# A graph network's attention loop: transposes and a small product moved to the end of a step, a row normalisation moved one step on

## The reference, cut to what matters

```python
    os1 = ssp(os1)                          # layer 3, scalar part; ssp(x) = softplus(x) - log 2
    os2 = os1 @ w_f2o2_s / math.sqrt(B)     # "the scalars' second product", B = 128
    ...                                     # x3 = layernorm(x2 + layer 3)
    q, k, v = jnp.split(x @ W, [Fqk, 2 * Fqk], axis=-1)      # layer 4, x is x3, H = 8 heads
    aw = jnp.einsum('ehf,ehf->eh', q[src] * scaling, k[dest])
    m = jax.ops.segment_max(aw, src, num_segments=n)
    e = jnp.exp(aw - m[src])
    denom = jax.ops.segment_sum(e, src, num_segments=n)
    out = jax.ops.segment_sum((e / denom[src])[:, :, None] * v[dest], src, num_segments=n)
x = _layernorm(x + out)
```

## Time and profile before

| | us |
|---|---|
| median of 3 runs | 2155.89 |
| lowest, highest | 2150.03, 2163.36 |
| the profiled execution's own time | 2165.3 |
| its span, first to last instruction | 2163.5 |
| PE busy | 1853.0 (86%) |
| DVE busy | 1442.2 (67%) |
| ACT busy | 1157.3 (53%) |

### The profile page before, as it was taken

How to read it: one execution, slowest core, us unless ns; L and a number is a source line. 1 busy time by engine, 2 the same in 40 slices (tenths; PEclk the granted TensorE clock), 3 DMA queues, 4 the chain that set the end, 5 groups by cost and what they waited for, 6 DMA issues and landing times. The chain is left out here.

```text
span 2163.5 us, 24571 instructions
## 1 busy us (share of the span) xinstructions
PE 1853.0 (86%) x5525; PEld 953.6 (44%) x5525; DVE 1442.2 (67%) x2642; ACT 1157.3 (53%) x2376; POOL 916.6 (42%) x1049
## 2 busy tenths in 40 slices
PE   5999999599999999999999995952881878888885
PEld 2444444244444444444444443521781444444442
DVE  5365555077777777777777774327985687788774
ACT  1344434255555555555555552224884888778772
POOL 2212102156666666666666663444553222232214
PEclk9999999799999999999999998975555887787777
DMA  7752102534444444444444445554556877777743
GB/s 251 246 206 67 25 10 31 141 133 171 171 164 164 158 164 171 171 167 161 167 156 171 171 147 199 98 93 156 113 111 189 244 223 222 223 221 215 225 133 119
DMA packets 165550, 344.68 MB, mean 159 GB/s; under 512 B 30146, under 2 KB 30627, under 8 KB 164966
## 3 DMA queue, kind: packets, MB, share of 16 engines
q1 hardware_dynamic: 130710, 247.28, 32.6%
q0 software_dynamic: 31424, 92.08, 19.0%
q10 hardware_dynamic: 3344, 4.51, 0.7%
HBM read 171.91 MB, written 153.71 MB: 151 GB/s over the span
## 5 line engine op out<-in xcount | busy, mean ns | idle before, releaser
L687 PE MATMUL d_p_h<-w3a,d_xT 128*128 128x512 f32 x632 | 286.4, 596 | 23.1 <-DMA d_xT<-in_xT 23.1
L687 PE MATMUL d_p_o<-d_w,d_uT 128*128 128x512 f32 x632 | 284.5, 593 | 3.0 <-ACT d_uT L762 3.0
L687 PE MATMUL d_p_p<-d_wr,d_x1T 128*128 128x512 f32 x632 | 285.1, 594 | 0.0
L562 POOL TENSOR_SCALAR d_small<-d_mv 128x1 f32<-128x1 f32 x158 | 78.0, 494 | 297.5 <-DVE d_mv L813 149.5
L851 DVE TENSOR_TENSOR d_zz<-d_yg,d_xbeta 128x512 f32<-128x512 f32 x79 | 136.9, 1733 | 96.2 <-POOL d_yg L902 96.2
L687 PEld LDWEIGHTS d_p_h<-w3a,d_xT 128*128 128x128 f32 x632 | 120.9, 192 | 176.0 <-issue 176.0
L687 PEld LDWEIGHTS d_p_o<-d_w,d_uT 128*128 128x128 f32 x632 | 119.8, 190 | 153.8 <-issue 149.2
L755 ACT ACTIVATE d_yn<-d_y,d_small 128x512 f32<-128x512 f32 x79 | 64.3, 814 | 228.4 <-POOL d_small L567 228.4
L1739 PE MATMUL f_p_qv<-filters,same_dst 128*128 128x512 f32 x160 | 126.4, 962 | 66.8 <-ACT same_dst L1819 66.8
L687 PEld LDWEIGHTS d_p_p<-d_wr,d_x1T 128*128 128x128 f32 x632 | 114.5, 191 | 114.4 <-issue 114.4
L783 ACT ACTIVATE d_x<-d_zz,d_small 128x512 f32<-128x512 f32 x79 | 64.2, 813 | 176.6 <-POOL d_small L567 176.6
(11 more groups left out here) (285 smaller groups left out, 4110.3 us busy)
## 6 DMA issues: line engine op xcount, KB each, us to landing
sum_counted<-m_tile_sum SPq DMA_DIRECT2D x10, 2112.0 KB, 7.8
state<-d_empty SPq DMA_DIRECT2D x80, 264.0 KB, 2.4
update<-d_empty SPq DMA_DIRECT2D x80, 256.0 KB, 2.3
pair_x<-x SPq DMA_DIRECT2D x40, 512.0 KB, 4.2
out_rows<-pair_rows SPq DMA_DIRECT2D x40, 512.0 KB, 3.7
d_xT<-in_xT SPq DMA_DIRECT2D x79, 256.0 KB, 2.7
d_z<-sum_counted SPq DMA_DIRECT2D x79, 256.0 KB, 2.8
d_x<-in_x SPq DMA_DIRECT2D x79, 256.0 KB, 3.1
```

The source lines that it names most:

```text
L562: nc.gpsimd.tensor_scalar(tmp, var, factor, add, ALU.mult, ALU.add).then_inc(done, 1)
L687: last = nc.tensor.matmul(out[:, :], lhsT[:, c, :], w[:, c, :], start=(c == 0), stop=(c == KB - 1))
```

## The change

On PE, the softplus transpose and the second product are now those of tile `a` (in the step in which its softplus is made), and the x3 transposes are those of tile `b` (in the step in which the rows are normalised). All of them stand after the keys and ahead of the tile sums. On ACT, their copies stand after `x3_rows(b)`, ahead of the step's last `tile_normalise`. `source_rows` runs for tile `e - 1`, one step later than before, and stands right after `state_factors(e)`. No instruction is added or removed; DVE, POOL and SP keep their lists.

```diff
@@ tensor
-                b, c, d = step - 1, step - 2, step - 3
-                if 0 <= c < T:
-                    turn_x3(c, 0)
-                    turn_x3(c, 1)
-                if 0 <= b < T:
-                    turn_ssp(b)
+                a, b, c, d = step, step - 1, step - 2, step - 3
                 if 0 <= c < T:
...
                     queries(c)
                 if 0 <= d < T:
                     turn_scores(d)
-                if 0 <= b < T:
-                    second(b)
-                if 0 <= d < T:
                     spread_scores(d)
                     values(d)
                 if 0 <= c < T:
                     keys(c)
+
+                if a < T:
+                    turn_ssp(a)
+                if 0 <= b < T:
+                    turn_x3(b, 0)
+                    turn_x3(b, 1)
+                if a < T:
+                    second(a)
                 if 0 <= d < T:
                     tile_sums(d)
@@ scalar
                 if 0 <= d < T:
                     away_from(d)
-                if 0 <= c < T:
-                    x3_turned_out(c, 0)
-                    x3_turned_out(c, 1)
                 if 0 <= e < T:
                     state_factors(e)
-                if 0 <= b < T:
-                    ssp_turned_out(b)
+                if 0 <= e - 1 < T:
+                    source_rows(e - 1)
...
                 if 0 <= d < T:
                     scores_out(d)
-                if 0 <= b < T:
-                    second_product_out(b)
...
                     x3_rows(b)
-                if 0 <= e < T:
-                    source_rows(e)
+                if a < T:
+                    ssp_turned_out(a)
+                if 0 <= b < T:
+                    x3_turned_out(b, 0)
+                    x3_turned_out(b, 1)
+                if a < T:
+                    second_product_out(a)
                 for u in range(unit + early + between, unit + TILES[step]):
                     tile_normalise(nc, k, act, u)
```

## The result

| | before | changed |
|---|---|---|
| median, us | 2156.65 (4 runs, 2150.03 to 2163.36) | 2223.61 (4 runs, 2223.36 to 2226.96) |
| ratio of the times | | 1.0314, 95% interval 1.028 to 1.0348 |
| profiled execution, us | 2165.3 | 2223.53 |
| span, us | 2163.5 | 2221.8 |

The kernel became slower, by the mechanism that was forecast and by more than was forecast: 2206 was predicted, with a range up to 2220, and 2223.61 came.

A forecast was written before the change was run, and what follows sets the result against it. Bound: PE's wait for ACT's x3 copies, behind DVE's attended row, in a 23.87 us step. +48 over 16 steps, +4 and -2 at the ends make +50: 2215 on the profiled execution, 2206 us on the median's footing; range 2174 to 2220.

The forecast's parts named there:

- The bound before, and the wait that goes: PE at the queries: 3.7 us of idleness and 6.7 of queries leave the critical chain, if nothing else were late.
- ACT's factors are late next: ACT at the factors: waits 1.6 us a step for DVE's f_fall, which ends 9.64 us after the weighing.
- Queued behind the factors: ACT from factors to score copy: 7.44 us, so the spread starts no sooner than 17.1 after the weighing.
- The clock behind it: PE after a 7.5 us gap: spread 3.5 and values 6.1 at low clock, period 26.9, +48 over 16 steps.
- The ends: Outside the sixteen steps: +4 us for the step ahead of them, -2 at the other end.
- The sum and its footing: Whole kernel: +48 + 4 - 2 = +50; 2215 us on the profiled 2165.3, 2206 on the median of 2155.89.
- The range: Whole time: 2174 to 2220 us; values between 5.19 and 6.56 and a spread between 3.0 and 4.0 give 2183 to 2222.
- A: Rival, PE's clock stays up in the loop: period 22.8 us, a gain of 17, time 2137; chance 0.06.
- B: Rival, the removed wait is paid out as factors are ready when ACT comes: step 20.5 us, time 2102; chance 0.07.
- C: Rival, only the values on PE are slow, not the spread, or values rise soonest: period 24.5 us, time 2168; chance 0.09.

The follow-up runs named there:

- Experiment 1: Changed kernel with one swap on ACT: source rows of the step before stand ahead of the factors instead of behind them; 2191.93 us, ratio 1.0145 to the kernel before.
- experiment 2: Changed kernel with source rows put back to tile e, right behind the x3 rows, moved transposes kept; 2192.95 us, ratio 1.014 to the kernel before.
- experiment 6: Kernel before with only the source rows one step later, behind the factors; transposes and second product not moved; 2217.73 us, ratio 1.0253.
- experiment 3: Changed kernel plus 14 unread products of 256 columns on PE between score transpose and spread; 2184.85 us, ratio 1.0106 to the kernel before.
- experiment 7: Changed kernel plus 17 unread products on PE in the gap ahead of the spread; 2172.76 us, ratio 1.0049 to the kernel before.
- experiment 8: Changed kernel with ACT reordered: query and score copies right behind the factors, then source rows and two plain tiles, two tiles at the end; 2149.35 us, ratio 0.9941.
- experiment 9: The new ACT order of experiment 8 with the plain tiles half a step sooner; 2121.66 us, ratio 0.981 to the kernel before.

## Why the prediction was right or wrong, point by point

- **The bound before, and the wait that goes.** Right: PE's wait at the queries went, and the queries run at full clock, from 5.66 to 9.26 us after the weighing (5.7 to 9.2 forecast).
- **ACT's factors are late next.** Right: 1.57 us a step, 1.6 forecast. Experiment 1 removed the wait by order alone and moved the spread by the source rows' 1.6.
- **Queued behind the factors.** Right: the spread comes 17.04 after the weighing (17.1), in experiments 1, 2 and 6 at 15.45, 15.62 and 17.30 (15.4, 15.6, 17.3).
- **The clock behind it.** The mechanism is right (experiments 3 and 7). Two terms of the sum were low: the spread took 3.71, not 3.5, and the values 6.36, not 6.1. That makes a period of 27.31 instead of 26.9, and over the 16 steps +55.1 (2156.77 - 1719.76 = 437.0 against 381.9) where the sum had +48. The slow spread lies between its bounds of 2.0 and 4.0; it was scaled from a spread of which only the last 0.71 us ran slowly. The estimate of 3.8 worked out from the ratio of 1.91 for 128 columns (the Trainium skill, "TensorE: Matmul & The Clock Gate", section "Back-to-back issue gap") was nearer: 3.71 / 1.98 is 1.87.
- **The ends.** This step failed most for its size: +2 was forecast, +9.2 came. *Start:* +4 was forecast. From the first logarithms (1654.73 before, 1648.72 after) to the first of the 17 spreads it took 64.1 before and 71.0 after: +6.9. The step that was priced came near, 24.26 instead of 19.77, +4.5. The other 2.4 lie ahead of its spread (44.4 and 46.8 us from the logarithms) and were not in the sum. There ACT now stands at the end of a step waiting for PE's slow transposes and second product, where plain tiles lay between before. In the first step of the changed kernel:

```profile
1651.59 0.38 ACT L1836 ACTIVATE f_sspT<-f_p_O 128x256 f32<-128x256 f32 x1 [1.56 <-PE f_p_O L1723]
1653.29 0.39 ACT L1842 ACTIVATE f_y<-f_p_R 128x256 f32<-128x256 f32 x1 [1.31 <-PE f_p_R L1733]
```

  The first of these waits is in the kernel before too, also 1.56; the second is new, and so are three short ones in each of the next two steps, 0.75 a step. Two waits of the kernel before, 0.35 and 0.66, are gone. That is 1.8 more of waiting, and one copy more stands ahead of the first spread.

  *End:* -2 was forecast, +2.3 came (62.7 us from the last full spread before, 65.0 after). The spread behind it was as early as forecast, 20.24 after the one before it (20.3), partly by luck: spread and values took 10.3 and not 9.8, and ACT's part 9.97 and not 10.5. But an earlier spread did not bring an earlier end. The end hangs on POOL's list of scatters, which goes on from the scatter of a merged state. Before and after, in that order, the first two of these scatters:

```profile
2119.41 0.97 POOL L1669 DMA_INDIRECT state<-f_new,unique  x1 [18.86 <-DVE f_new L2027]
...
2136.20 0.97 POOL L1669 DMA_INDIRECT state<-f_new,unique  x1 [1.60 <-DVE f_new L2027]
```

```profile
2177.15 0.97 POOL L1669 DMA_INDIRECT state<-f_new,unique  x1 [20.95 <-DVE f_new L2027]
...
2194.40 0.96 POOL L1669 DMA_INDIRECT state<-f_new,unique  x1 [0.30 <-issue]
```

  The first comes 18.6 and 20.4 after the last full spread: that step's own spread and values are slow now (+2.9), and 1.1 of it is won back behind the weighing. From it to the end of the span are 44.1 and 44.7 us. Before, POOL waited once more, 1.60 us, for the merge behind the spread at 2122.63. In the changed kernel it doesn't, so the spread at 2177.01 could not have brought the second scatter sooner. (Further on, at 2209.81, the chain over the last spreads meets POOL's list once more, within 0.1 us.) I followed PE where POOL sets the end.
- **The sum and its footing.** +50 against +64.3 measured within the loop (+55.1, +6.9, +2.3). The traces' spans differ by 58.3, as the changed kernel's loop happened to begin 6.0 sooner: at 1648.72, where the other ten traces have 1651.7 to 1657.6. The forecast of 2206 also took 9.4 off, for a median of three runs that later runs did not bear out; against 2164 the same sum gives 2214, and a range moved up by the same 8 would have held the time. So the miss of 17.6 is made of a sum too small by 14.3 (7.1 in the sixteen steps, 7.2 at the ends) and the 9.4 of the footing, less the 6.0 of an early loop, which was luck.
- **The range.** It took in values at 6.56 and a spread at 4.0 as far as 2222, and was then cut at 2220. Errors of the ends were not in it at all.
- **The rivals.** A (the clock stays up) is refuted: it fell in every step. Its price was wrong too, 22.8 a step where experiment 7 measured 23.17. What the Trainium skill says of this ("TensorE: Matmul & The Clock Gate", section "HAM oscillation") has two halves: to join a loop's PE work keeps the clock warm, and a gap inside the loop makes each round start slowly. In the changed kernel only the second showed: PE's work is joined but for one gap of 7.4 us, and each spread starts at 1.2 GHz. B (the wait is paid out) didn't occur in the changed kernel, but experiments 8 and 9 show how most of it is had: by giving the chain from `f_fall` to the score copy no other work (2149.35), and then the plain rows' buffers sooner (2121.66; B was put at 2102). C (only the values slow) is what a partly filled gap gives: 24.46 in experiment 3, where 24.5 was worked out.

## What to carry to other kernels

When a wait is removed, follow every instruction that now stands in front of the next cross-engine hand-over, and ask what that engine waits for there: here 1.6 us of source rows and 4.9 of two plain tiles stood between DVE's result and PE's start. An in-order list should hand over first and fill up afterwards. Price TensorE's work by the clock that it will meet in its new place, and weigh the beginning and the end of a loop by the list that really ends them, with a footing from as many runs as there are.

## What the runs showed of the hardware that was not expected

Filling a gap by work that nobody reads makes the kernel faster (51 us in experiment 7). Still, the granted clock fell from 1.00 to 0.50 behind the spread at 1915.19 with PE busy throughout, and not behind the one at 1939.63, with the same products ahead of it. Whether the spread's small products have to do with it was not tried apart.

Different chains gave the same period. In the changed kernel 17.04 and values at 6.36, in experiment 6 17.30 and values at 6.09, both give 27.31 in step after step: what the chain gained, the values lost to the clock. The kernel before stands at 23.89 in two traces. Experiment 1, in between, never settled (25.8, 24.8, 24.5 in turn). So a change of some tenths of a us in such a chain may cost or bring nothing.

The kernel before ranges from 2140.62 to 2169.69 over its runs beside the experiments, while the four runs of the changed one lie within 4 us. This goes with TensorE's clock: the runs of the kernel before under 2150 us have a mean granted clock of 0.897 to 0.905, those over 2168 us 0.886 to 0.889. Why it is granted more in some executions was not found.
